# Dealing VectorE's small steps out between the input products and scans, and moving the z projection next to gating

## What is computed

```python
h = layernorm(x) * (1 + ca) + sa
xz = h @ in_proj.T;  xc = silu(conv(xz_x));  z = xz_z          # 256 channels each
dt, B, C = split(xc @ x_proj.T);  delta = softplus(dt @ dt_w.T + dt_b)
state[t] = state[t-1] * exp(delta * A) + delta * xc * B        # 256 x 16 states, 512 steps
y = (sum_n state * C + xc * D) * silu(z)
x = x + ga * (y @ out_proj.T)
h = layernorm(x) * (1 + cb) + sb
p = softmax(h @ router + b);  keep the two largest of 8 (ties: the lower index first)
x = x + gb * (shared_expert(h) + sum_e w_e * expert_e(h))      # gelu between two products
```

## Time and profile before

| what | us |
|---|---|
| median of 3 runs | 691.35 (687.95 to 692.08) |
| the profiled execution, its time | 692.83 |
| its span in the profile | 691.1 |
| busy: TensorE / VectorE / ScalarE / GpSimd | 603.8 / 598.5 / 486.4 / 320.2 |
| VectorE's largest groups: scans, input products | 292.2, 157.6 |

### The profile page before, as it was taken

How to read it: one execution, slowest core, us unless ns; L and a number is a source line. 1 busy time by engine, 2 the same in 40 slices (tenths; PEclk the granted TensorE clock), 3 DMA queues, 4 the chain that set the end, 5 groups by cost and what they waited for, 6 DMA issues and landing times.

```text
span 691.1 us, 9751 instructions
## 1 busy us (share of the span) xinstructions
PE 603.8 (87%) x3646; PEld 472.4 (68%) x3646; DVE 598.5 (87%) x713; ACT 486.4 (70%) x861; POOL 320.2 (46%) x171
## 2 busy tenths in 40 slices
PE   6776378999899999999999998999999957998897
PEld 4234344789466965788577956797578946698686
DVE  5399999999999999999999999999997999797416
ACT  3588643899579984999389966999389923973360
POOL 1026556445644556445553655446543664464000
PEclk9978579999999999999999999999999968999999
DMA  7324234314432235133431343223521442220000
GB/s 218 133 115 141 121 138 144 119 62 158 169 105 110 90 130 195 62 123 123 172 121 62 123 160 135 84 100 124 169 108 67 177 154 74 110 77 16 1 1 15
DMA packets 26704, 77.85 MB, mean 113 GB/s; under 512 B 3025, under 2 KB 17570, under 8 KB 18466
## 3 DMA queue, kind: packets, MB, share of 16 engines
q1 hardware_dynamic: 26178, 76.82, 31.0%
q10 hardware_dynamic: 480, 0.43, 0.2%
HBM read 74.61 MB, written 2.62 MB: 112 GB/s over the span
## 4 chain that ended last, share of the span: by engine, by line
PE 46%; DVE 25%; ACT 18%; issue 7%; POOL 2%; DMA 1%; DVEq 0%; POOLq 0%; ACTq 0%
DVE state L1207 12%; PE psum L516 7%; ACT decay L886 6%; DVE psum L1198 6%; PE psum L545 6%; PE psum L678 5%; ACT gT_mix L981 5%; PE psum L646 5%; PE psum L648 4%; PE psum L647 4%; PE psum L663 2%; PE psum L567 2%; POOL state L433 1%; ACT L867 1%; PE psum L594 1%
## 5 line engine op out<-in xcount | busy, mean ns | idle before, releaser
L433 POOL TENSOR_TENSOR state<-state,bc 128x1024 f32<-128x1024 f32 x127 | 300.1, 2363 | 298.1 <-DVE psum L1198 298.1
L1207 DVE TENSOR_TENSOR_SCAN state<-decay,psum 128x1024 f32<-128x1024 f32 x128 | 292.2, 2283 | 22.1 <-PE psum L516 9.6
L886 ACT ACTIVATE decay<-delta,a_neg 128x511 f32<-128x511 f32 x256 | 166.7, 733 | 10.4 <-DVE state L1207 10.3
L516 PE MATMUL psum<-ident,state 128*128 128x128 f32 x1024 | 141.7, 286 | 28.8 <-POOL state L433 28.8
L1198 DVE TENSOR_TENSOR psum<-bc,du 128x1024 f32<-128x1024 f32 x128 | 157.6, 1231 | 4.8 <-DVE state L1207 0.5
L516 PEld LDWEIGHTS psum<-ident,state 128*128 128x128 f32 x1024 | 122.9, 148 | 51.0 <-POOL state L433 38.8
L678 PE MATMUL psum<-down_w,h 128*128 128x128 f32 x896 | 109.9, 276 | 0.0
L678 PEld LDWEIGHTS psum<-down_w,h 128*128 128x128 f32 x896 | 104.4, 192 | 5.3 <-issue 5.3
L1015 ACT ACTIVATE h<-psum,vec 128x512 f32<-128x512 f32 x144 | 97.0, 689 | 2.9 <-PE psum L648 1.4
L981 ACT ACTIVATE gT_mix<-psum,w 128x128 f32<-128x128 f32 x224 | 65.3, 400 | 8.0 <-PE psum L688 6.4
L545 PE MATMUL psum<-h_sb,conv_in_wT 128*128 128x512 f32 x128 | 62.8, 639 | 9.2 <-ACT h_sb L896 9.2
(11 more groups left out here) (151 smaller groups left out, 664.1 us busy)
## 6 DMA issues: line engine op xcount, KB each, us to landing
bc<-bc_rows SPq DMA_DIRECT2D x64, 1024.0 KB, 4.7
x_sb<-_attn_hidden_states_dram SPq DMA_DIRECT2D x9, 256.0 KB, 2.8
x<-_attn_hidden_states_dram SPq DMA_DIRECT2D x7, 256.0 KB, 3.1
out_dram<-out_sb SPq DMA_DIRECT2D x7, 256.0 KB, 2.4
h<-in_L_ffn_rw_dram SPq DMA_DIRECT2D x1, 1024.0 KB
bc_rows<-rows SPq DMA_DIRECT2D x8, 64.0 KB, 3.6
h<-in_L_wmod_dram ACTq DMA_DIRECT2D x1, 384.0 KB
h<-in_L_attn_in_proj_w_dram SPq DMA_DIRECT2D x1, 256.0 KB, 4.5
```

The lines of the kernel that those rows point to most:

```text
L433: pool.tensor_tensor(state[:, u % STATE_RING, :, :], state[:, u % STATE_RING, :, :], bc[:, pair % BC_RING, 1, first:first + NU, :], ALU.mu ...
L516: last = nc.tensor.matmul(Y[q][:, t * P:(t + 1) * P], state[:, u % STATE_RING, s, t * P:(t + 1) * P], ident[:, :], start=False, stop=(u in ...
L886: last = nc.scalar.activation(decay[:, r, s, 1:L], delta[:, b.p, q, 1:L], ACT.Exp, scale=a_neg[:, q, k:k + 1])
L1207: nc.vector.tensor_tensor_scan(state[:, u % STATE_RING, :, :].rearrange("p n t -> p (n t)"), decay[:, u % DECAY_RING, :, :].rearrange("p n ...
```

## The change

VectorE's list for a slot with scans is written out unit by unit (`scan_slots`). The small steps that stood in groups are cut into single steps and put one or two at a time between an input product and its scan, or behind a scan. `finish` of the batch before moves from input 15 to behind scan 0 of the next slot, and its store and the residual load move to the head of SP's list there. The statistics of the first layer norm are taken at units 12 to 15 of the slot before (the x load comes earlier for it), the normalization in units 2 to 5. Top-2 marks ties by comparing each probability with a table-scaled copy (`tie_scale`), which takes two steps of 128x256 less. On TensorE z_proj moves from between y_add(0) and y_add(1) to between y_add(15) and g_transpose; dt_proj, which shares its PSUM banks, waits for z_gate; y_add(3) moves behind the third up; x_transpose moves ahead of the third down. On ScalarE z_gate follows bcdt_rows, the exp table is loaded ahead of att_rows, decays of units 6 and 7 stand ahead of h2_rows and those of 8 and 9 behind it, all ahead of the gelu run; before, 6 and 7 stood ahead of it. The diff, cut to what the text speaks of (of the new `scan_slots` only the new lines; the removed ones are the old order told above):

```diff
+            def store(a):
+                sp.wait_ge(out_done, a.i + 1)
+                sp.dma_start(out[a.i].rearrange("(t p) d -> p t d", p=P),
+                             out_sb[:, :, :]).then_inc(out_stored, 16)
+
             def slots(b, a, n, m):
-                first_batch = n and isinstance(n.i, int) and n.i == 0
-                if m and first_batch:
+                if m and not b and n:
                     sp.wait_ge(xT_done, m.i)
                     load_x(m)
+                if a and a.i > 0:
+                    store(Batch(a.i - 1, 1 - a.p))
+                if a:
+                    load_residual(a)
                 if n:
                     sp.wait_ge(bcdt_done, n.i + 1)
                     sp.dma_start(bc_dram[n.i], bcdt[0:2 * NS, :]).then_inc(bc_stored, 16)
                     sp.wait_ge(bc_stored, n.i * 16 + 16)
-                if m and n and not first_batch:
-
-                    load_x(m)
                 if b:
                     load_bc(b, 2)
                     load_bc(b, 3)
-                if n:
-                    load_bc(n, 0)
+                if b and m and m.i + 1 < B:
+                    sp.wait_ge(xT_done, m.i + 1)
+                    load_x(Batch(m.i + 1, 1 - m.p))
                 if b and is_last(b):
                     sp.wait_ge(xT_done, B)
                     load_residual(b)
-                if a:
-                    sp.wait_ge(out_done, a.i + 1)
-                    sp.dma_start(out[a.i].rearrange("(t p) d -> p t d", p=P),
-                                 out_sb[:, :, :]).then_inc(out_stored, 16)
-                if b and not is_last(b):
-
-                    load_residual(b)
-                if n:
+                if n:
+                    load_bc(n, 0)
                     load_bc(n, 1)
+                if m and not b and n:
+                    sp.wait_ge(xT_done, m.i + 1)
+                    load_x(Batch(m.i + 1, 1 - m.p))
                 if b and b.i == 1:
                     sp.wait_ge(gate_steps, 4)
                     sp.dma_start(gate_dram, gateT[:, 1, B - 1:B]).then_inc(gate_stored, 16)
...
 
             def tail(a):
+                store(Batch(a.i - 1, 1 - a.p))
...
@@ -437,13 +443,15 @@
             def slots(b, a, n, m):
                 if a:
                     readout(a, UN - 1, paced=b is not None)
+                if m and (a or not b):
+                    make_rstd(0, stats_done, rstd_eps, rstd_done, m)
                 for u in range(UN - 1):
                     if b:
                         readout(b, u)
+                    if m and b and not a and u == 1:
+                        make_rstd(0, stats_done, rstd_eps, rstd_done, m)
                     if a and u == 2:
                         make_rstd(1, stats2_done, rstd2_eps, rstd2_done, a)
-                    if m and u == 5:
-                        make_rstd(0, stats_done, rstd_eps, rstd_done, m)
...
             def z_proj(n, half):
                 if n.i > 0:
-                    pe.wait_ge(sp_abs, Q * n.i + half + 1)
+                    pe.wait_ge(xb_done, Q * n.i + half + 1)
...
             def dt_proj(n, q):
                 pe.wait_ge(bcdt_done, n.i + 1)
+                pe.wait_ge(zs_done, 2 * n.i + q + 1)
                 nc.tensor.matmul(A[q], dt_wT[2 * NS:2 * NS + R, q, :],
...
             def keep_busy(a, n, count):
 
                 if n:
-                    pe.wait_ge(zs_done, 2 * n.i + 2)
+                    pe.wait_ge(sp_abs, Q * n.i + Q)
...
                 if a:
                     y_add(a, UN - 1)
+                if n and n.i > 0:
+                    z_proj(n, 0)
+                    z_proj(n, 1)
                 if a:
                     g_transpose(a, n)
                 if b and a:
@@ -733,9 +743,6 @@
                     dt_proj(n, 1)
                 if b and a:
                     y_add(b, 0)
-                if n and n.i > 0:
-                    z_proj(n, 0)
-                    z_proj(n, 1)
...
@@ -746,10 +753,11 @@
                 if a:
                     keep_busy(a, n, 5 if b else 12)
                     router(a)
-                    for k in range(M_UP):
+                for k in range(M_UP):
+                    if a:
                         up(a, n, k)
-                if b:
-                    y_add(b, 3)
+                    if b and k == 2:
+                        y_add(b, 3)
...
                 if b:
                     y_add(b, 6)
                 for u in range(8, UN - 2):
+                    if m and u == 8:
+                        x_transpose(m, n, a)
                     for j in MIX_AT[u]:
                         if a and j + 2 < DOWNS:
                             down(a, j + 2)
                         if a:
                             mix_add(a, j)
-                    if m and u == 10:
-                        x_transpose(m, n, a)
...
                     bcdt_rows(n)
-                    if n.i == 0:
-                        z_gate(n, 1)
+                    if n.i > 0:
+                        z_gate(n, 0)
+                    z_gate(n, 1)
                 if a:
                     g_rows(a, n)
+                if a:
+                    load_exp_table(a)
                     att_rows(a)
                 for q in range(Q):
                     if n:
                         softplus_relu(n, q)
                         softplus_abs(n, q, b)
-                if n and n.i > 0:
-                    z_gate(n, 0)
-                    z_gate(n, 1)
                 if n:
                     softplus_exp(n, a)
-                if a:
-                    load_exp_table(a)
-                    h2_rows(a)
                 if b:
                     decays(b, AHEAD)
                     decays(b, AHEAD + 1)
+                if a:
+                    h2_rows(a)
+                if b:
+                    decays(b, AHEAD + 2)
+                    decays(b, AHEAD + 3)
                 if a:
                     router_e(a)
                     load_gelu_table(a)
...
+            def tie_bars(a):
+                dve.wait_ge(prob_step, 6 * a.i + 3)
                 nc.vector.tensor_tensor(
-                    gt_eq[:, 1, :, :, :], gt_eq[:, 1, :, :, :],
-                    before[:, :, :].unsqueeze(1).broadcast_to([P, NT, E, E]),
+                    gt_eq[:, 1, :, :, :], pr[:, :, :].unsqueeze(3).broadcast_to([P, NT, E, E]),
+                    tie_scale[:, :, :].unsqueeze(1).broadcast_to([P, NT, E, E]),
                     ALU.mult).then_inc(prob_step, 1)
...
+            def beaten(a):
+                dve.wait_ge(prob_step, 6 * a.i + 4)
+                nc.vector.tensor_tensor(
+                    gt_eq[:, 0, :, :, :], pr[:, :, :].unsqueeze(2).broadcast_to([P, NT, E, E]),
+                    gt_eq[:, 1, :, :, :], ALU.is_gt).then_inc(prob_step, 1)
...
-                if b:
-                    decays(b, AHEAD + 2)
                 for j in range(DOWNS - 1):
-                    if b:
-                        decays(b, AHEAD + 3 + j)
+                    if b and j < DOWNS - 2:
+                        decays(b, AHEAD + 4 + j)
...
+            def scan_slots(b, a, n, m):
+                late = Batch(m.i + 1, 1 - m.p) if m and m.i + 1 < B else None
+                new = m if b.i == 0 else None
+                old = m if b.i > 0 else None
+
+                scan_input(b, 0)
+                if new:
+                    bn_x(new, 0)
+                    bn_x(new, 1)
+                if old:
+                    aggr_x(old)
+                scan(b, 0)
+                if a and a.i > 0:
+                    finish(Batch(a.i - 1, 1 - a.p))
+
+                scan_input(b, 1)
+                if new:
+                    bn_x(new, 2)
+                    bn_x(new, 3)
                 if a:
                     gate_y(a)
+                scan(b, 1)
+
+                scan_input(b, 2)
+                if new:
+                    aggr_x(new)
+                if old:
+                    xhat(old, 0)
+                scan(b, 2)
+
+                scan_input(b, 3)
                 if a:
                     residual(a)
+                if old:
+                    xhat(old, 1)
+                if a:
+                    stats2(a)
+                scan(b, 3)
                 if a:
                     x1hat(a)
+
+                scan_input(b, 4)
+                if new:
+                    xhat(new, 0)
+                    xhat(new, 1)
+                if old:
+                    xhat(old, 2)
+                scan(b, 4)
                 if a:
                     split_h2(a)
                     logits(a)
+
+                scan_input(b, 5)
+                if new:
+                    xhat(new, 2)
                 if m:
+                    xhat(m, 3)
+                scan(b, 5)
+                if a:
+                    prob_sum(a)
+                if n:
+                    relu_plus_exp(n)
+                if a:
+                    prob_inverse(a)
+
+                scan_input(b, 6)
+                if a:
```

(54 more changed lines are left out.)

165 lines of the change are left out of this document (73 added, 92 removed).

## The result

| what | us |
|---|---|
| median of 4 runs after | 702.78 (701.59 to 709.17) |
| median of 4 runs before, on the same chip | 690.05 (687.95 to 692.08) |
| ratio after to before | 1.0202, 95% interval 1.0159 to 1.0245 |
| the profiled execution after, its time / its span | 702.04 / 699.4 |
| busy after: TensorE / VectorE / ScalarE / GpSimd | 606.4 / 591.8 / 489.0 / 334.0 |

Slower by 2%, where 679.5 was forecast. The experiments ran on three chips, on which the kernel before had medians of 692.34 (e1 to e4), 689.37 (e5 to e8) and 690.44 us (e9 to e12), so ratios are to be compared, not times.

What follows compares the result with a forecast made beforehand. TensorE was taken to bound the second half of a middle batch, a chain from gate_y (start: G) the first; slot gains of 2.5 + 2.0 + 3.2 + 3.3 + 0.9 = 11.9 us gave 680.9 profiled, 679.5 median, range 675 to 684.

Steps and rivals of the forecast that it cites:

- step 2: Middle slots, VectorE: four xhat steps in four gaps, two ahead of x1hat, add 0.3 us to the chain to the first up.
- Step 8: Middle slots, queues: later residual load and x loads are covered; moving make_rstd between GpSimd's readouts costs 0.
- the clock: Rival, chance 0.12: joined TensorE holes let the clock fall once in each of six slots, 1.7 us each: 689.7.
- Hiding of 0.25 a gap: VectorE: a gap that gets its first small step hides 0.25 us; 12 more gaps in a middle slot, 3.0 us.
- TensorE not the bound: Rival, chance 0.15: VectorE's gain comes through, middle slots take 72.7 us, 2.1 less for each of five slots: 669.
- Nothing hidden: Rival, chance 0.15: each VectorE step dealt out costs its full length; the gains sum to 4.1 us: 687.
- The slower rival: Chance 0.06: the low clock lasts and takes in two up runs, 10.6 us more each: 700.7.
- Step 1: Middle slots, TensorE: z_proj fills the hole ahead of g_transpose; about 1.5 us of hole reopens ahead of x1_transpose; gain 0.
- Steps 3 and 4: Middle slots: moved decays leave the gelu run's start, gain 0; y_add(3) behind the third up brings weights_transpose to G+31.8, gain 0.25.
- Step 5: Middle slots: top-2 weights ready at G+31.4, TensorE wants them at G+31.8; gain 0, 0.4 us to spare.
- Step 7: Middle slots: ScalarE's lead makes the last mix product ready when TensorE comes, removing a wait of 0.52 us.
- Step 6: Middle slots, VectorE: rounded_exp waits 3 us for the log behind the gelu run, covered by 2 us.

Runs made afterwards that it cites:

- e1: Kernel after, with unit 3's xhat step moved ahead of the residual and batch 0's four steps one to a gap: 689.03 us, ratio 0.996.
- e4: Kernel before with only the change's TensorE and ScalarE part (z_proj, z_gate, y_add(3), exp table, decays): 684.62 us, ratio 0.9914.
- e5: Kernel after, with GpSimd making rstd for x1hat ahead of the readout of unit 2 instead of behind it: 706.69 us, ratio 1.0241.
- e8: Kernel after, with z_proj, z_gate, exp table and decays back in their old places, y_add(3) left: 713.87 us, ratio 1.0361.
- e9: Kernel before, with only its four xhat steps moved from behind scan 6 to between input 8 and scan 8: 706.47 us, ratio 1.0227.
- e12: e6 with the four xhat steps one each directly behind inputs 4, 5, 6 and 7 in every slot: 688.36 us, ratio 0.9965.
- e6: Kernel after with the edit of e1 and the gate row stored one slot earlier: 682.43 us, ratio 0.9893.
- e3: Kernel after with 42 instead of 14 filling matmuls without use ahead of x1_transpose: 702.99 us, ratio 1.0163.
- e7: e6 with 28 instead of 14 filling transposes ahead of x1_transpose: 682.7 us, ratio 0.9892.

## Why the prediction was wrong

**The step that failed is step 2**, "Four xhat steps stand in four gaps, two of them ahead of x1hat: +0.3". One of the two is not first in its gap and took 2.03 us. Step 8's "On GpSimd ... 0" is the same omission from the other side: it looked at what GpSimd waits for, not at what its readouts do to others. A second step failed beside it, step 8's "residual is three units later: covered", for the second slot: the load came 3.61 us late. And the sum had nothing for the clock, which stood among the rivals alone. Hiding of 0.25 a gap was right for what it was read from (after, the step at 274.21 puts scan 2 at 1.40 behind its input, a bare one is at 1.37, so 0.31 of its 0.34 are hidden), but it holds only for the first step, or for a kind that doesn't mind the readout. The rows of before couldn't show it by themselves: every tensor_scalar there stood behind a scan, when the readout was over the earlier trace rows, and GpSimd's own order of time was not read. It should have been, since the change moves work into the very stretches in which GpSimd is busy. The Trainium skill has the rule ("SBUF — State Buffer", Who interferes with whom): GpSimd shares VectorE's second pair of SBUF ports as an exclusive lock for a whole instruction; a VectorE tensor_scalar in a two-port mode contends for it, and so does an op with two SBUF inputs when GpSimd's instruction reads SBUF; whichever issues first has it and the other fully blocks. The traces agree on what is held: 0.34 against 2.03, 2.62 and 2.65 us, 0.19 against 2.43, and residual, bn_stats and scan not held. In which mode the tensor_scalar ran, and that ports are what the two share, no trace shows.

**The sum, redone** on the profiled execution (forecast 680.9, measured 702.04):
- collision in the first, third, fourth and fifth slot: x1_transpose at G+15.36 instead of the G+13.80 of e6, 1.56 each: 6.2;
- second slot: G+17.38 instead of G+13.80, the late load: 3.6. Step 8 had called the residual load covered, and had not followed SP's list to the slot in which it stands still for the gate row;
- the clock, from x1_transpose to weights_transpose against 17.74: 2.73 + 0.27 + 1.56 + 2.75 + 1.58 = 8.9;
- up to the first G: 112.02 against 109.0, 3.0. The head of this execution was shorter by luck: the first rounded_exp (L1184, L1174 before) starts at 33.20, at 35.37 before and in e3, whose code is the same up to there and whose first G is at 114.51. From that step to the first G it is 78.8 us after and 79.1 in e3, 74.2 in e6, 76.1 before and 73.6 by the forecast: 4.6 for the two pairs, 0.6 not gained, 2.2 of luck off;
- the late slots: 0.8 and 0.5 better than forecast, -1.3; around the span 2.6 instead of 1.7, +0.9.

Together 21.3 of the 21.1 us. The line of the clock takes every difference from 17.74 as the clock's; the sixth slot, at a clock of 1.00, has 18.07 there, so up to 0.3 a slot may be something else.

**Rivals.** TensorE not the bound: refuted for the kernel after, by the wait of 2.13 at gate_y, and by e6, whose third slot has all of VectorE's saving and takes 74.75. Nothing hidden: refuted by the scans that follow a first step 1.40 behind their input. The section of the Trainium skill that the prediction sets against its rows ("VectorE: DVE Perf Modes", The DRAIN you can't avoid) also says that a next op that isn't held starts earlier, so the 1.15 us of an independent successor don't contradict it; the 1.40 in place of 1.37 does contradict a reading by which only the count of instructions matters. The clock: 1.7 us once in each of six slots was the price; it fell in five, at 0.3 to 2.75. It makes 8.9 of the 21.1 us. In e6 and e7, without the collision and the late load, it costs 0 to 0.5 in most middle slots and 1.6 where it falls in the ups, so most of it went with them; but the larger hole isn't its condition, since it fell with the hole filled (e3) and once with a hole of 1.75 (e4, fourth slot, 19.30 us from x1_transpose to weights_transpose). What decides when it falls isn't settled. The slower rival, a low clock through two up runs (700.7), came near the measured time by luck: the low stretches after are at most some 10 us, and an up run at half clock alone would take 21.

**Point by point.** Step 1 right: no hole ahead of g_transpose, and e4 shows the hole of 1.75 ahead of x1_transpose. Steps 3 and 4 right: fourth up and weights_transpose at their places once x1hat is (G+20.96 and G+31.54 in e6, G+21.2 and G+31.8 forecast). Step 5 right: the weights come at G+31.28 in e6 (31.4 forecast) and weights_transpose doesn't wait for them; in e12, where they come later, it does. Step 7 right: the hole ahead of the last mix_add is gone, and back in e8. Step 6 right in kind: rounded_exp waits 4.37 us after, not 3, since the gelu run ends later with the ups (2.81 in e6's third slot), and it is covered (VectorE after):

```profile
308.24 0.69 DVE L1184 TENSOR_SCALAR g_soft<-g_soft 128x1024 f32<-128x1024 f32 x1 [4.37 <-ACT skip L966]
308.85 2.28 DVE L1222 TENSOR_TENSOR_SCAN state<-decay,psum 128x1024 f32<-128x1024 f32 x1
```

Of its own signs of being wrong one came: the clock fell in most batches. The other two did not (weights_transpose waited for nothing, no middle slot fell below 74).

Without the two failures the sum nearly holds: middle slots of 74.75 in e7 against 74.8, and 682.4 against 679.5 in all. Most of what is still missing lies in the first expert slot (76.8 and 76.2 instead of 74.8): in e6 the residual waits 1.49 us for its load there too (at 118.02), now that the first G is 4 us sooner. "Covered" failed once more. The slower side, at 0.06, was priced far too low: one unpriced resource shared by two engines and one load called covered were enough.
